# A transformer block on one Trainium2 core: the products of the first attention in rounds of four 32-column matmuls

## The reference

```python
b, tq, _ = query.shape                       # query = layernorm(x); key = value = ctx, 2 x 154 x 128
q = (query @ Wq.T + bq).reshape(b, tq, NUM_HEADS, HEAD_DIM).transpose(0, 2, 1, 3)   # 16 heads of 8
k = (key @ Wk.T + bk).reshape(b, tk, NUM_HEADS, HEAD_DIM).transpose(0, 2, 1, 3)
v = (value @ Wv.T + bv).reshape(b, tk, NUM_HEADS, HEAD_DIM).transpose(0, 2, 1, 3)
scores = jnp.einsum('bhqd,bhkd->bhqk', q, k) / np.sqrt(HEAD_DIM)
attn = jax.nn.softmax(scores, axis=-1)
out = jnp.einsum('bhqk,bhkd->bhqd', attn, v).transpose(0, 2, 1, 3).reshape(b, tq, EMBED_DIM)
return out @ Wo.T + bo
```

## Time and profile before

| | |
|---|---|
| median of 3 runs | 317.59 us (313.51 to 318.61) |
| the profiled execution | 317.64 us, of which 315.8 us are the span of its instructions |
| busy in that span | PE 271.5 us (86%), DVE 204.8 us, ACT 133.1 us, POOL 81.3 us |
| mean granted TensorE clock | 0.945 of full speed |

### The profile page before, as it was taken

The page is one execution under the profiler, slowest core; times in us unless marked ns, Lnnn a source line. Parts: engine busy times, 40 slices in busy tenths (PEclk is TensorE's granted clock), DMA queues, the critical chain, the costliest instruction groups (busy, mean ns, idle before and its releaser), DMA issues.

```text
span 315.8 us, 3845 instructions
## 1 busy us (share of the span) xinstructions
PE 271.5 (86%) x1216; PEld 185.8 (59%) x1226; DVE 204.8 (65%) x498; ACT 133.1 (42%) x254; POOL 81.3 (26%) x96
## 2 busy tenths in 40 slices
PE   0688879999999877588999977979699999999994
PEld 0465445645546442144777854956368888888882
DVE  1584743636756778877843516764747888888884
ACT  1555314444353326012424424744335656555552
POOL 3461532080002028000007002020003454355410
PEclk9989979999999997959999999898859999999999
DMA  7950000000000000000001200000001212211001
GB/s 249 430 210 0 2 0 0 1 0 2 1 0 0 2 0 0 1 2 0 0 2 34 68 2 1 0 2 0 0 0 33 49 54 67 67 39 61 0 0 66
DMA packets 4433, 11.41 MB, mean 36 GB/s; under 512 B 761, under 2 KB 1081, under 8 KB 4162
## 3 DMA queue, kind: packets, MB, share of 16 engines
q1 hardware_dynamic: 4114, 10.46, 10.0%
q10 hardware_dynamic: 304, 0.76, 0.7%
HBM read 10.69 MB, written 0.52 MB: 36 GB/s over the span
## 4 chain that ended last, share of the span: by engine, by line
PE 67%; DVE 19%; issue 6%; ACT 4%; DMA 2%; POOL 2%; ACTq 0%; DVEq 0%; POOLq 0%
PE bank L1115 9%; PE bank L1400 5%; PE bank L1401 5%; PE bank L1402 5%; PE bank L1006 3%; DVE att L564 3%; PE bank L1072 3%; PE bank L1012 3%; PE bank L1408 3%; PE bank L1439 3%; DVE arena_b L620 3%; PE bank L1442 2%; PE bank L1440 2%; PE bank L1303 2%; PE bank L1102 2%
## 5 line engine op out<-in xcount | busy, mean ns | idle before, releaser
L1115 PE MATMUL bank<-arena_c 128*128 128x512 f32 x80 | 42.2, 612 | 1.2 <-ACT osb L807 1.2
L968 ACT ACTIVATE arena_d<-bank,bias 128x512 f32<-128x512 f32 x34 | 23.4, 689 | 38.1 <-PE bank L1402 38.1
L733 DVE SCALAR_TENSOR_TENSOR arena_d<-bank,bias,arena_d 128x512 f32<-128x512 f32 x34 | 25.5, 751 | 16.7 <-PE bank L1408 16.7
L852 ACT ACTIVATE arena_c<-bank 128x512 f32<-128x512 f32 x40 | 23.9, 597 | 23.1 <-PE bank L1103 23.0
L274 POOL TENSOR_TENSOR rstd<-vareps,neghalf 128x4 f32<-128x4 f32 x10 | 10.1, 1010 | 89.2 <-DVE vareps L420 89.2
L1102 PE MATMUL bank<-arena_a 128*128 128x512 f32 x40 | 31.1, 777 | 0.9 <-issue 0.7
L459 DVE TENSOR_REDUCE smax<-bank 128x8 f32<-128x1232 f32 x16 | 22.9, 1439 | 13.3 <-PE bank L1072 13.3
L361 POOL CAST arena_b<-rec 128x512 fp32r<-128x512 f32 x17 | 16.7, 984 | 56.2 <-PE bank L1442 46.4
L1012 PE MATMUL bank<-pack,onesb 128*128 128x512 bf16 x98 | 28.8, 427 | 0.5 <-issue 0.2
L1400 PE MATMUL bank<-arena_b 128*128 128x512 f32 x68 | 28.0, 412 | 0.0
L1401 PE MATMUL bank<-arena_b 128*128 128x512 f32 x68 | 27.4, 404 | 0.0
(11 more groups left out here) (243 smaller groups left out, 545.5 us busy)
## 6 DMA issues: line engine op xcount, KB each, us to landing
rec<-in_rec SPq DMA_DIRECT2D x17, 257.0 KB, 2.6
arena_d<-in_fc SPq DMA_DIRECT2D x1, 2048.0 KB, 10.3
fc<-in_fc SPq DMA_DIRECT2D x1, 2048.0 KB, 14.7
x<-in_x SPq DMA_DIRECT2D x2, 256.0 KB, 5.5
out<-x SPq DMA_DIRECT2D x2, 256.0 KB, 2.0
pack<-in_pack ACTq DMA_DIRECT2D x1, 396.0 KB, 4.5
watt<-in_watt SPq DMA_DIRECT2D x1, 384.0 KB, 6.1
ctx<-in_ctx ACTq DMA_DIRECT2D x1, 308.0 KB, 6.6
```

Of the source, the lines that this page charges most:

```text
L733: dve.scalar_tensor_tensor(gu[:, c, :], bank[:, 2 + c, :], bias[:, u, 1:2], sil[:, c, :], ALU.add, ALU.mult).then_inc(Z["gu_ready"], 1)
L852: act.activation(pT[:, n % 3, :], bank[:, 3 + n % 2, :], ACT.Exp, scale=float(DH) ** -0.5)\
L968: act.activation(sil[:, c, :], bank[:, c, :], ACT.Silu, bias=bias[:, u, 0:1]).then_inc(Z["sil_ready"], 1)
L1115: ins = pe.matmul(bank[:, 5, :], vaug[:, b, g, i, :], pT[:, n % 3, :], start=(i == 0), stop=(i == NBLK - 1))
```

## The change

`attend` no longer multiplies ten blocks of 128 positions by 128 columns. The 8 heads are split in two halves of 4 heads (616 positions, padded to five blocks each), and the ten blocks are taken as four **pairs of heads**, each of which touches three blocks, so 12 products of 128 positions by 32 columns (16 value columns, 2 columns of ones, 14 of zeros). Pair `j` writes partitions 32j to 32j + 31 of bank 5. They are issued in three rounds of four, one for each pair (`ROUNDS`: pair, its block, the place of that block in the order of scores); `ORDER` is the order in which the ten blocks' scores are made. `pT` has eight slots in place of three. A round stands behind score 6 and two behind score 10.

The output is copied to `osb` as before, then **turned** on TensorE (`out_turned`, four 128 x 128 transposes), divided with tokens in partitions (a reciprocal of 128 x 32 and a product of 128 x 256), and once both head groups are in, turned back (`back_turned`); `bv` and `Wo` are permuted to the new order of channels. The end of combination 3 does this in two halves (`last_out_turned`, `last_back_turned`).

Both halves of heads see the same five windows of values, so `values` makes five matmuls for a sequence, not ten. On POOL the masked values are 4 x 96 columns and not 2 x 640, the ones 384 and not 2 x 640.

The **order** changes too: on DVE the norm of the second sequence's `x` comes before the maxima of combination 1, and in the end the norm of `y0` into `xn` and the mask copy `keep` come behind the second sequence's statistics; on POOL `x + bo` comes one combination later; the rough tiles of combination 0 come before the values; the scores are no longer a block ahead of `attend`, and at a boundary the transposes for the maxima and the queries stand between the last two rounds; the projection of sequence 0 moves from combination 2 to 3; ten and two `idle_work` before the last projection are gone, and the rest writes bank 5.

```diff
-FLAT = HH * SK
-NBLK = -(-FLAT // P)
+HALF = HH // 2 * SK
+HBLK = -(-HALF // P)
+NBLK = 2 * HBLK
+SPAN = NBLK // 2 * P + HALF
...
-ROUGH_AT = (1, 3, 6, 7)
+ROUGH_AT = (1, 3, 5, 7)
+ORDER = (0, 3, 5, 8, 1, 4, 6, 9, 2, 7)
+ROUNDS = (((0, 0, 0), (1, 1, 1), (2, 0, 2), (3, 1, 3)),
+          ((0, 1, 4), (1, 2, 5), (2, 1, 6), (3, 2, 7)),
+          ((0, 2, 8), (1, 0, 8), (2, 2, 9), (3, 0, 9)))
+RING = 8
 
 SECOND_PICKS = {0: (0, 2), 1: (2, 5), 2: (5, T)}
-VGROUPS = ((0, 4), (4, 8), (8, NBLK))
+VGROUPS = ((0, 4), (4, HBLK))
...
-        vraw, vaug, pT = lay(arena_c, ([P, NBLK, D], [P, B, 2, NBLK, P], [P, 3, S]))
+        vraw, vaug, pT = lay(arena_c, ([P, HBLK, D], [P, B, 2, 12, 32], [P, RING, S]))
...
-            def normalise(c, c0=0, c1=S):
+            def normalise(c, part=None):
 
                 g = c % 2
-                own, other = slice(g * HW, (g + 1) * HW), slice((1 - g) * HW, (2 - g) * HW)
-                dve.wait_ge(Z["osb_ready"], c + 1)
-                if c >= 2:
-                    dve.wait_ge(Z["attT_ready"], 1)
-                link(dve.reciprocal(att[own, c0:c1], osb[other, c0:c1]))
-                dve.tensor_tensor(att[own, c0:c1], osb[own, c0:c1], att[own, c0:c1], ALU.mult)\
+                dve.wait_ge(Z["aq_psum"], c + 1 + (part or 0))
+                if c == 2:
+                    dve.wait_ge(Z["at_psum"], 1)
+                i0, i1 = (0, TB) if part is None else (2 * part, 2 * part + 2)
+                turned_ = bank[:, 7 if part is None else (6, 2)[part], i0 * P:i1 * P].rearrange("p (n c) -> p n c", c=32)
+                to = att[:, i0 * P:i1 * P].rearrange("p (n g h d) -> p n g h d", g=2, h=2, d=DH)[:, :, g]
+                n = 4 * (i1 - i0)
+                link(dve.reciprocal(rden[:, 4 * i0:4 * i1, :], turned_[:, :, 2 * DH:2 * DH + 2]))
+                dve.tensor_tensor(to, turned_[:, :, 0:2 * DH].rearrange("p n (h d) -> p n h d", h=2),
+                                  rden[:, 4 * i0:4 * i1, :, None].broadcast_to([P, n, 2, DH]), ALU.mult)\
                     .then_inc(Z["att_ready"], 1)
...
             q_lo(0)
             for i in range(TB):
                 maxima(0, i)
+            dve.wait_ge(L["x1"], 16)
+            norm(x, xn, TB, "xn_ready")
...
             for c in range(COMBOS):
                 if c + 1 < COMBOS:
                     for i in range(TB):
-                        if c and i == 1:
+                        if c and i == 2:
                             normalise(c - 1)
                         maxima(c + 1, i)
-                        if c == 0 and i == 1:
-                            dve.wait_ge(L["x1"], 16)
-                            norm(x, xn, TB, "xn_ready")
                     if c + 2 < COMBOS:
...
             center(n, x1, y0, 0, "y0_ready")
             dve.wait_ge(Z["gsum_ready"], 1)
             gate_shift(0, n)
-            dve.wait_ge(Z["y0_ready"], TB)
-            norm(y0, xn, 0, "yh_ready")
-            dve.wait_ge(L["mask"], 16)
-            dve.tensor_scalar(keep[:, :, :], mask[:, :, :], 0.0, None, ALU.is_equal).then_inc(Z["keep_ready"], 1)
+            for part in range(2):
+                normalise(COMBOS - 1, part)
             gate_scores(0)
-
-            dve.wait_ge(Z["osb_ready"], COMBOS + 1)
-            link(dve.reciprocal(osb[:, 0:S // 2], osb[:, 0:S // 2]))
-            for a, rows in enumerate((slice(0, HW), slice(HW, P))):
-                cs = slice(a * S // 2, (a + 1) * S // 2)
-                dve.tensor_tensor(att[HW:P, cs], bank[HW:P, 5, cs], osb[rows, 0:S // 2], ALU.mult)\
-                    .then_inc(Z["att_ready"], 1)
             norms[0] += 1
             n = norms[0]
             for a in range(2):
...
                     ins = dve.bn_stats(stats[:, (n - 1) % 2, i, :], x1[:, TB + i, :])
             link(ins)
             aggregate(n)
+            dve.wait_ge(Z["y0_ready"], TB)
+            norm(y0, xn, 0, "yh_ready")
             gate_shift(1, n)
             gate_scores(1)
             center(n, x1, y0, TB, "y0_ready")
             dve.wait_ge(Z["y0_ready"], T)
             measure(y0, TB)
-
+            dve.wait_ge(L["mask"], 16)
+            dve.tensor_scalar(keep[:, :, :], mask[:, :, :], 0.0, None, ALU.is_equal).then_inc(Z["keep_ready"], 1)
 
             dve.wait_ge(Z["srep_ready"], 2)
...
-                    if n >= 3:
-
-                        act.wait_ge(*((Z["o_psum"], (n - 2) // NBLK) if (n - 2) % NBLK == 0 else
-                                      (Z["pv_done"], n - 2 - (n - 3) // NBLK)))
+                    if n >= RING:
+                        act.wait_ge(Z["pv_done"], len(ROUNDS) * ((n - RING) // NBLK) + (n - RING) % NBLK // 4 + 1)
...
-                    if c + 1 < COMBOS and i == 8:
+                    if c + 1 < COMBOS and i == NBLK - 1:
                         minus_max(c + 1)
+                    if c + 2 < COMBOS and i == NBLK - 1:
+                        queries(c + 2)
...
-            def attend(c, i):
-
-                b, g, n = c // 2, c % 2, c * NBLK + i
-                if i == 0:
-                    pe.wait_ge(Z["vaug_ready"], 2 * (b + 1))
-                    pe.wait_ge(Z["ones_ready"], 2 * (b + 1))
+            def attend(c, r):
+
+                b, g = c // 2, c % 2
+                if r == 0:
+                    pe.wait_ge(Z["vaug_ready"], 4 * (b + 1))
+                    pe.wait_ge(Z["ones_ready"], b + 1)
                     if c:
                         pe.wait_ge(Z["osb_ready"], c)
-                pe.wait_ge(Z["exp_done"], n + 1)
-                ins = pe.matmul(bank[:, 5, :], vaug[:, b, g, i, :], pT[:, n % 3, :], start=(i == 0),
-                                stop=(i == NBLK - 1))
-                ins.then_inc(Z["o_psum"] if i == NBLK - 1 else Z["pv_done"], 1)
+                pe.wait_ge(Z["exp_done"], c * NBLK + ROUNDS[r][-1][2] + 1)
+                for j, s, at in ROUNDS[r]:
+                    ins = pe.matmul(bank[32 * j:32 * j + 32, 5, :], vaug[:, b, g, 3 * j + s, :],
+                                    pT[:, (c * NBLK + at) % RING, :], start=(r == 0), stop=(r == len(ROUNDS) - 1))
+                ins.then_inc(Z["pv_done"], 1)
+
+            def out_turned(c):
+                pe.wait_ge(Z["mT_ready"], c + 2)
+                pe.wait_ge(Z["osb_ready"], c + 1)
+                for i in range(TB):
+                    ins = turn(bank[:, 7, i * P:(i + 1) * P], osb[:, i * P:(i + 1) * P])
+                ins.then_inc(Z["aq_psum"], 1)
+
+            def back_turned(b):
+                take6(Z["attT_ready"], b + 1)
+                pe.wait_ge(Z["att_ready"], 2 * (b + 1))
+                for i in range(TB):
+                    ins = turn(bank[:, 6, i * P:(i + 1) * P], att[:, i * P:(i + 1) * P])
+                ins.then_inc(Z["at_psum"], 1)
+
+            def last_out_turned(part):
+                if part == 0:
+                    take6(Z["att_ready"], COMBOS)
+                else:
+                    pe.wait_ge(Z["lgsub_ready"], 1)
+                pe.wait_ge(Z["osb_ready"], COMBOS + part)
+                for i in (2 * part, 2 * part + 1):
+                    ins = turn(bank[:, 2 if part else 6, i * P:(i + 1) * P], osb[:, i * P:(i + 1) * P])
+                ins.then_inc(Z["aq_psum"], 1)
+
+            def last_back_turned(part):
+                pe.wait_ge(Z["att_ready"], COMBOS + part)
+                for i in (2 * part, 2 * part + 1):
+                    ins = turn(bank[:, part, i * P:(i + 1) * P], att[:, i * P:(i + 1) * P])
+                ins.then_inc(Z["at_psum"], 1)
 
...
-            rough(0, 0)
-            for r in range(3):
-                rough(0, r + 1)
+            for i in range(TB):
+                rough(0, i)
+            for r in range(2):
                 values(0, r)
             maxima(0)
-            scores(0, 0)
-            queries(1)
             for c in range(COMBOS):
                 for i in range(NBLK):
-                    if c * NBLK + i + 1 < COMBOS * NBLK:
-                        scores(c + (i + 1) // NBLK, (i + 1) % NBLK)
-                    if c + 1 < COMBOS:
-                        if i in ROUGH_AT:
-                            rough(c + 1, ROUGH_AT.index(i))
-                    if c == 0 and i == 8:
+                    scores(c, i)
+                    if c == 0 and i == 0:
+                        queries(1)
+                    if i == 5:
+                        attend(c, 0)
+                    if c + 1 < COMBOS and i in ROUGH_AT:
+                        rough(c + 1, ROUGH_AT.index(i))
+                    if c and i == 3:
+                        out_turned(c - 1)
+                    if c == 0 and i == 4:
                         turned(1)
-                    if c == 1 and i in (2, 4, 6):
-                        values(1, i // 2 - 1)
+                    if c == 1 and i in (4, 6):
+                        values(1, (i - 4) // 2)
                     if c == 2 and i == 7:
+                        back_turned(0)
+                    if c == 3 and i == 1:
                         project(0)
```

(66 more changed lines are left out.)

134 lines of the change are left out of this document (73 added, 61 removed).

## The result

The changed kernel takes 297.67 us (median of 4 runs, 297.04 to 300.03) against 317.9 us (median of 4, 313.51 to 318.61) for the kernel before beside it. The profiled execution takes 297.29 us, with a span of 295.5 us.

A forecast was written before the change was run, and what follows sets the result against it. TensorE was taken to bound the four combinations. From 317.6 us, 21.1 us came off for the attention (80.4 to 59.8 us, and 0.5 us at the start) and 2.3 us were added at the end: 299 us, range 293 to 313.

The forecast's parts named there:

- A round: In attend, four products run side by side with some loss: 1.1 us, against 0.86 us at full overlap.
- Combinations 1 to 3: Attention windows after the first: 20.9, 19.2 and 14.9 us fall to 16.0, 15.2 and 11.8 us, rounds' loss included.
- the same waits: Combination 2, boundary and rough-tile waits as in combination 1: 1.3 us added.
- Combination 0: First attention window: 25.5 us falls to 16.0 us, or 16.7 us with the rounds' loss.
- less 1.7: Combination 0: the four us at clock 0.57 behind the old gap return to full clock, 2.3 us.
- new waits of 2.0 and 0.7 us: Combination 0: TensorE waits 2.0 us for the queries' low part, then 0.7 us in all for reductions.
- the chain of maxima: Rival: maxima waits at the combination boundaries show fully, or a half-clock stretch comes: 304 to 309 us; chance 0.12, with clock.
- a fall of the clock for more than 4 us inside the combinations: Sign in the attention windows that, if seen, would show the prediction wrong.
- The end: Last block to first count: 12.9 us before, 1.4 less for steps, 2.6 more for y0's norm, 0.8 for keep; plus 2.3.
- The first count: Behind the attention: comes some 15 us after the last round, with nothing changed from the counts on.
- The staircase: Rival: matmuls start strictly in order, so a round takes five steps of 0.43 us, 2.15 us; 311.4 us; chance 0.25.
- One behind another: Rival: products of 32 columns do not overlap, a round takes 3.44 us; 327 us, slower; chance 0.10.

The follow-up runs named there:

- experiment 1: The changed kernel with all four products of a round writing one column group: 327.14 us, ratio to the kernel before 1.042.
- experiment 3: The changed kernel with each round's four products issued twice: 307.51 us.
- experiment 6: The changed kernel with idle_work added in TensorE's gaps ahead of and inside the first scores: 292.45 us, ratio to the kernel before 0.926.
- experiment 4: The kernel before with only the second sequence's norm moved early and x + bo one combination later: 313.14 us, ratio 0.994.
- experiment 2: The changed kernel with its new order but ten products over 128 columns a combination: 317.34 us, ratio to the kernel before 1.008.
- experiment 5: The changed kernel with y0's statistics and the mask copy put ahead of the last division: 294.03 us, ratio to the kernel before 0.929.
- experiment 7: The changed kernel with both the y0 statistics and mask copy moved early and the idle_work in the first gaps: 288.19 us, ratio to the kernel before 0.914.

## Why the prediction was right

The predicted time was 299 us, the measured 297.67. The mechanism that brings the gain was right; that the sum came so near is in part luck. By its own steps:

**A round** was put at 1.1 us, and is 0.99; experiments 1 and 3 show the overlap and that the loss (0.13 us) is paid once, not per product. The 1.1 us were too cautious, by 1.3 us over twelve rounds. (The prediction has 1.1 us also as three quarters of the way to full overlap; three quarters of the way from 3.44 to 0.86 us are 1.5 us, so that support does not hold.)

**Combinations 1 to 3**, with their rounds, were put at 16.0, 15.2 and 11.8 us; they are 15.1, 14.15 and 11.3. Here the line of additions and subtractions on TensorE, with the waits that its shorter line lays bare, was right to about 1 us each, always on the high side, 2.4 us in all. (Combination 2 has 1.3 us for "the same waits" that were 0.8 and 0.3 in combination 1.)

**Combination 0** is the term that was mis-sized: 16.7 us forecast, 20.9 measured. The step that failed is "less 1.7, since the four us at clock 0.57 would be 2.3 at full clock". I took away the slow stretch behind the old gap and did not put one behind the new waits of 2.0 and 0.7 us, although I had named it beside the chain of maxima. The prediction named a fall of the clock for more than 4 us inside the combinations as a sign that it is wrong, and this sign came: the clock was down in most of the time from 14 to 39 us, and inside combination 0 for about 10 us (a mean of 0.75 over 20.9 us, split into half and full clock). That also brought the first scores 0.8 us later than before, where they were put 0.5 us earlier, and with ACT's copies waiting for slow matmuls the low part of the queries came at 29.26 and not at 27.0 (at 27.97 in experiment 6, at full clock). Experiment 6 takes only the gaps away, by work that nobody reads, and the forecast 16.7 us stand in its window. A gap does not always bring the clock down: the profiled execution of experiment 4 has one of 1.89 us at the same place and kept full clock from 24 to 118 us. In the changed kernel and in experiments 1, 2, 3 and 5, which all have its short waits close together there, the clock fell between 25 and 39 us every time. What exactly brings it down is not shown; that filling the gaps keeps it up stands in the traces of experiments 6 and 7.

**The end** was put at 12.9 + 2.3 = 15.2 us and is 15.45. Both costs that I named are there, and experiment 5 takes them away, 3.45 us for 3.4. DVE waited for the power between statistics and centring, as forecast (1.12 us).

**The first count** was so forecast at 98.8 us and came at 101.9. Nothing should have changed behind it, and yet that stretch fell from 198.2 to 193.6 us, which covers the miss. The instructions there are the same in all nine kernels whose traces there are, but for the bank of some `idle_work`. The windows from the first count to the end, of the kernel before, the changed one, and experiments 1, 4 and 7, one fence each:

```profile
117.59:315.80 198.21, 175.53 (x851) 128.68 (x860) 136.38 (x364) 84.90 (x169) 48.47 (x66) 0.93 0.08 22
```

```profile
101.91:295.50 193.59, 172.22 (x860) 125.61 (x860) 136.34 (x363) 84.73 (x169) 48.44 (x66) 0.95 0.08 22
```

```profile
129.36:327.00 197.64, 175.96 (x860) 127.77 (x860) 136.38 (x363) 85.04 (x171) 48.44 (x66) 0.93 0.08 22
```

```profile
115.31:307.00 191.69, 170.41 (x860) 124.83 (x860) 136.44 (x364) 84.89 (x169) 48.47 (x66) 0.96 0.08 23
```

```profile
92.52:284.50 191.98, 169.72 (x860) 123.39 (x860) 136.42 (x364) 84.76 (x169) 48.52 (x66) 0.97 0.08 23
```

DVE's busy time is 136.4 us in each, ACT's and POOL's the same within 0.4; the length follows the mean clock, 198.2 and 197.6 us at 0.93, 191.7 and 192.0 at 0.96 and 0.97. The other four, experiments 2, 3, 5 and 6, have 197.4, 192.1, 195.3 and 196.4 us at 0.94, 0.95, 0.95 and 0.94. A kernel of the old products (experiment 4) has the short stretch too. So nothing gives the 4.6 us to the change: they are where the slow clock happens to fall, and one profiled execution of either kernel could have had them or not. The forecast started from 317.6 us, near the upper end of what the kernel before takes (312.1 to 318.6 us over all its runs). That the sum came within 1.3 us is luck: a miss of 3.1 us, and this one in the other direction.

**The rivals.** The staircase needed five steps of 0.43 us. The starts show two: the first passes of all four pairs start together, although the second pass of pair 0 is a separate instruction, as 80 matmuls for 40 products were before. From that row alone, the list of passes could also be in another order than I assumed. Experiment 1 decides it. Its last two rounds follow one another, each in a column group of its own, and the second waits for a semaphore of its own. One behind another their sixteen passes would take 16 x 0.43 = 6.9 us. The chain, and the view of the line in the windows 110.37 to 110.4 us and 110.7 to 111.2 us:

```profile
108.68 5.31 PE bank L1124 x16
...
L1124 PE MATMUL bank<-arena_c x3: 592/592/617, 109.9 to 110.4; 128*32 128x512 f32 x3
L1124 PEld LDWEIGHTS bank<-arena_c x3: 106/109/110, 110.4 to 110.4; 128*32 128x32 f32 x3
...
L1124 PE MATMUL bank<-arena_c x4: 592/592/617, 110.4 to 110.8; 128*32 128x512 f32 x4
```

From 108.6 us on, passes start 0.43 us apart. At 110.4 us the fifth of the first round starts, and beside it already the first of the second round (the one of 617 ns, as at the start of a round): three weight loads there, and from then on two passes at a time. Three passes of the first round are still to come. So TensorE lets passes of another column group start ahead of older ones that wait, and the staircase's premise fails. Strict order of matmuls, as the Trainium skill states it in TensorE: Matmul & The Clock Gate, Part 3, does not hold for these passes. The 2.38 times that the same page of the Trainium skill has for three products are exceeded by four: 3.44 / 0.99 = 3.5 times.

One behind another is experiment 1, and it came out at the 327 us that the prediction gave it. The chain of maxima showed as the waits that were counted (each at most 0.61 us) and did not become the bound in combinations 1 and 2. But the other half of that rival, a stretch at half clock because TensorE has more gaps, is what happened in combination 0. The time stayed below the 304 us of that rival by the luck named above.

`x + bo` behind the values had less room than I said: it ended at 60.3 us, and the spreading of the keys behind it held one rough tile up, but for 0.37 us.

## What to carry to other kernels

Where many products have a stationary operand (the weights) of which only a quarter of the columns matters, put four of them in four column groups and issue them together: a round cost little more than one product here, 0.99 against 0.86 us, and the turns and waits of the new arrangement did not eat the gain. When TensorE's line is cut, ask two things of the profile again: what had been free beside it and now ends the stretch (here a norm and a copy, 3.4 us), and where its new gaps lie, since the clock can fall there (here 4.2 us in one combination). A difference of a few us in a stretch that holds the same instructions in both kernels is to be read with the clock column beside it before it is given to the change.

## What the runs showed that was not expected

A narrow round that follows another costs 0.86 us, as much as a single wide product, so what is lost of the four-fold overlap is 0.13 us, once. And the cheapest of the edits, 24 matmuls that nobody reads, gave at least as much as the reordering of the end: 292.45 against 294.03 us beside each other (the runs overlap), and in the traces 5.3 us against 3.45. Without them TensorE's clock was at its half level (1.2 of 2.4 GHz) for about 17 us of the first 40, if a mean of 0.57 over 8 us and of 0.63 over 14 us is split into half and full clock.
